# Two-layer graph network on one core: relation products in pairs by Strassen's 7 products for 8, the root product in 35 pieces, 75 edge columns placed by GpSimd's writes

## What is computed

```python
x = layernorm(x + gat_layers(x, src, dst, ...))          # two attention layers, then @ Wu
# relational layer
seg  = edge_type * n + dst
agg  = segment_sum(x[src], seg, 34 * n);  cnt = segment_sum(ones, seg, 34 * n)
mean = agg.reshape(34, n, -1) / maximum(cnt, 1).reshape(34, n, 1)
h1   = einsum('rni,rio->no', mean, W_rel) + x @ W_root + b_rgcn
xw   = h1 @ W_gcn                                         # then a degree-normalised sum over edges
x    = layernorm(x + (sum over edges of xw[src]*norm + xw*dinv^2 + b_gcn))
```

## Time and profile before

| | before |
|---|---|
| median of 3 runs | 3700.54 us |
| the profiled execution | 3701.15 us |
| its span, first to last instruction | 3699.4 us |
| PE / DVE / ACT / POOL busy, share of the span | 93 / 48 / 35 / 33 % |
| DMA | 397.58 MB, mean 107 GB/s |

### The profile page before, as it was taken

How to read it: one execution, slowest core, us unless ns; L and a number is a source line. 1 busy time by engine, 2 the same in 40 slices (tenths; PEclk the granted TensorE clock), 3 DMA queues, 4 the chain that set the end, 5 groups by cost and what they waited for, 6 DMA issues and landing times. The chain is left out here.

```text
span 3699.4 us, 64083 instructions
## 1 busy us (share of the span) xinstructions
PE 3458.5 (93%) x18811; PEld 2178.5 (59%) x18811; DVE 1769.7 (48%) x4227; ACT 1278.9 (35%) x2313; POOL 1227.8 (33%) x1373
## 2 busy tenths in 40 slices
PE   6989988866699999999999999999999998989998
PEld 3544457866466666666666666666666665444545
DVE  8999994767622122111123445544554432443324
ACT  2965535635222222222223444444444432000010
POOL 0000000000055544444502344334433411777771
PEclk9999999987899999999999999999999999999999
DMA  2010010000533333333334555555554544555551
GB/s 86 1 39 0 0 57 24 1 3 9 169 112 105 104 115 107 103 105 104 104 113 130 160 173 167 155 157 172 168 160 152 171 124 134 157 157 158 157 135 54
DMA packets 227146, 397.58 MB, mean 107 GB/s; under 512 B 39186, under 2 KB 179473, under 8 KB 227072
## 3 DMA queue, kind: packets, MB, share of 16 engines
q1 hardware_dynamic: 167226, 253.52, 20.2%
q0 software_dynamic: 57600, 141.81, 14.3%
q10 hardware_dynamic: 2246, 1.29, 0.1%
HBM read 254.24 MB, written 142.25 MB: 107 GB/s over the span
## 5 line engine op out<-in xcount | busy, mean ns | idle before, releaser
L1684 PE MATMUL bank<-arena 128*128 128x384 f16 (+1 forms) x4200 | 1372.1, 327 | 2.2 <-ACT arena L896 2.0
L1685 PE MATMUL bank<-arena 128*128 128x384 f16 (+1 forms) x4200 | 1370.8, 326 | 0.0
L1686 PE MATMUL bank<-arena 128*128 128x384 f16 (+1 forms) x4200 | 1370.8, 326 | 0.0
L896 ACT ACTIVATE arena<-bank,winv 128x384 f32<-128x384 f32 (+1 forms) x680 | 390.5, 579 | 1278.9 <-PE bank L1686 1257.9
L1684 PEld LDWEIGHTS bank<-arena 128*128 128x128 f16 (+2 forms) x4200 | 422.4, 101 | 274.6 <-issue 15.9
L1686 PEld LDWEIGHTS bank<-arena 128*128 128x128 f16 (+2 forms) x4200 | 422.4, 101 | 261.4 <-issue 1.5
L1685 PEld LDWEIGHTS bank<-arena 128*128 128x128 f16 (+2 forms) x4200 | 422.7, 101 | 258.9 <-issue 6.0
L605 POOL DMA_INDIRECT arena<-y_half,idx_now x360 | 401.5, 1115 | 145.1 <-issue 118.0
L589 POOL DMA_INDIRECT w_now<-rel_inv_dram,idx_now x360 | 379.2, 1053 | 155.7 <-issue 87.4
L1320 DVE TENSOR_TENSOR arena<-arena,bank 128x384 f32 x180 | 99.7, 554 | 625.0 <-PE bank L1664 382.8
L619 POOL DMA_INDIRECT arena<-y_half,idx_now x360 | 343.1, 953 | 131.3 <-issue 112.7
(11 more groups left out here) (218 smaller groups left out, 3626.3 us busy)
## 6 DMA issues: line engine op xcount, KB each, us to landing
y_half<-arena SPq DMA_DIRECT2D x612, 192.0 KB
arena<-in_L_gnn_W_rel_dram SPq DMA_DIRECT2D x68, 1152.0 KB, 7.1
arena<-y_half,idx_now POOLq DMA_INDIRECT x720, 3.3
y_half<-arena SPq DMA_DIRECT2D x68, 147.0 KB
w_now<-rel_inv_dram,idx_now POOLq DMA_INDIRECT x360, 2.7
arena<-in_x_dram SPq DMA_DIRECT2D x10, 384.0 KB, 7.3
arena<-in_L_gnn_b_rgcn_dram SPq DMA_DIRECT2D x10, 384.0 KB, 9.2
xu_dram<-arena SPq DMA_DIRECT2D x9, 384.0 KB, 2.6
```

The lines of the kernel that those rows point to most:

```text
L896: nc.scalar.activation(to, bank[n % RB][0:r, 0:CH], ACT.Copy, scale=winv[0:r, c:c + 1]).then_inc(r_copied, 1)
L1684: nc.tensor.matmul(acc, xh, w_hi[c][:, k, :], start=(k == 0), stop=False)
L1685: nc.tensor.matmul(acc, xh, w_lo[c][:, k, :], start=False, stop=False)
L1686: ins = nc.tensor.matmul(acc, xl, w_hi[c][:, k, :], start=False, stop=(k == KT - 1))
```

## The change

1. **Pairs.** A step is now a pair of relations. x1 is cut into 2 x 2 blocks (node tiles 0 to 4 and 5 to 9; depth blocks 0 to 2 and 3 to 5), the weights into 2 x 2 (depth halves; 192-column halves, both relations side by side, so that a product has 384 columns). Seven products (m = 1 to 7) of 5 tile pairs t, 9 matmuls each, replace 2 x 10 tiles of 18. Seven combinations of x1 are made once (`x1_sums`, `x1_high`, `x1_low`), the weight combinations per pair by GpSimd (`t1_t2`, `t3`, `t4`), four `tensor_tensor` of 128 x 1152. Products m = 1, 6, 5, 3 of a tile pair stand one upon the other in one bank, which is read in between; ScalarE copies out after m = 1, 7, 6, 3 (20 a step) and VectorE adds after m = 2, 5, 4 (15 a step).
2. **Weights.** One `w_raw` for the pair (both loads, 1152 KB each, go out when all 7 `low` of the step are done), seven slots of `w_hi`/`w_lo` of 128 x 1152, four maxima of 128 x 1152 instead of two of 128 x 2304.
3. **Edges.** Still six units per pair, for 15 pairs. `weigh` has two buffers, and its last copy (`weighed`) comes one unit later.
4. **Root product.** The same 35 products with W_root as the "pair"; they stand between the first units of the tail (5 before unit 0, then 3 for 2 units, done by unit 20). `cT` is stored to DRAM after the first attention layer and loaded again in the tail (10 DMAs), `hs` of half 1 is set at the tail's start.
5. **Sort.** SCAT = 75 of the 330 columns are left out of the one-hots; GpSimd writes each of their edges (8 bytes) to its place in DRAM with 75 indirect DMAs of 125 rows, SyncE loads the result (360 KB) and VectorE adds it. 17 rounds of 15 columns remain, and the 10 product pieces of L1434 are spread over them.

The diff, cut to its core:

```diff
-        SORT_PARTS = 11
-        SORT_STEPS = EC // NL // SORT_PARTS
+        SORT_STEPS = 1
+        SORT_PARTS = (EC - SCAT) // NL // SORT_STEPS
...
+        ORDER = [(m, t) for ts in ((0, 1), (2, 3), (4,)) for m in (1, 7, 6, 2, 5, 4, 3) for t in ts]
+        BANKS = [(0, 1, 2), (3, 4, 7), (2, 1, 0), (7, 4, 3), (4, 1, 0)]
...
+            pool.wait_ge(units_ready, 1)
+            for c in range(SCAT):
+                nc.gpsimd.indirect_dma_start(
+                    out=placed_dram, out_offset=bass.IndirectOffsetOnAxis(ap=place[:, c:c + 1], axis=0),
+                    in_=pay[:, c, :], in_offset=None).then_inc(edges_placed, 16)
...
+            def t3(q, i):
+                for j in range(2):
+                    pool.wait_ge(w_loaded[j], step(q, i) * 16 + 16)
+                nc.gpsimd.tensor_tensor(X1, B22, B12, ALU.subtract).then_inc(t_done, 1)
+            def t1_t2(q, i):
+                pool.wait_ge(w_max, step(q, i) * 4 + 2)
+                nc.gpsimd.tensor_tensor(B12, B12, B11, ALU.subtract).then_inc(t_done, 1)
+                pool.wait_ge(t_done, step(q, i) * 4 + 2)
+                nc.gpsimd.tensor_tensor(X2, B22, B12, ALU.subtract).then_inc(t_done, 1)
+            def t4(q, i):
+                pool.wait_ge(w_lo_ready, step(q, i) * 7 + LOW[1])
+                nc.gpsimd.tensor_tensor(B11, B21, X2, ALU.subtract).then_inc(t_done, 1)
...
+            def weights_step(q, i, next_q, next_i):
+                weigh(i, 0)
+                t4(q, i)
+                weigh(i, 1)
+                weighed(i, 0)
+                weigh(i, 2)
+                weighed(i, 1)
+                t3(next_q, next_i)
+                t1_t2(next_q, next_i)
+                largest(next_q, next_i)
+                weigh(i, 3)
+                weighed(i, 2)
+                weigh(i, 4)
+                weighed(i, 3)
+                weigh(i, 5)
+                weighed(i, 4)
+                weighed(i, 5)
...
+            # ScalarE, start of a step
+            def one_step(q, i, next_q, next_i, edges):
+                s = step(q, i)
+                if edges:
+                    edge_high(q - 1, i, PER, 0)
+                used_high(q, i, 5, B12, 2)
+                m1_out(s, 0)
+                used_high(q, i, 4, B11, 4)
+                m1_out(s, 1)
+                used_high(q, i, 3, B22, 0)
+                m7_out(s, 0)
...
+            # VectorE, a step, the edge_low / edge_add of six units left out
+                low(q, i, 2, B21)
+                low(q, i, 5, B12)
+                low(q, i, 4, B11)
+                low(q, i, 3, B22)
+                m2_add(s, 0, ybuf[0])
...
+                measure(next_q, next_i, 0)
+                measure(next_q, next_i, 1)
+                m2_add(s, 2, ybuf[2])
+                m2_add(s, 3, ybuf[3])
+                scale(next_q, next_i)
+                m5_add(s, 2, ybuf[2])
...
+            # TensorE, one product
+            def product(s, m, t):
+                for k in range(KH):                      # KH = 3
+                    nc.tensor.matmul(acc, h, w_hi[m - 1][:, k, :], start=fresh and k == 0, stop=False, ...)
+                    nc.tensor.matmul(acc, h, w_lo[m - 1][:, k, :], start=False, stop=False, ...)
+                    ins = nc.tensor.matmul(acc, l, w_hi[m - 1][:, k, :], start=False, stop=k == KH - 1, ...)
+            def m6(s, t):
+                weights(s, 6)
+                copied(s, 1, t)
+                product(s, 6, t)
...
+            # SyncE, a step
+                sp.wait_ge(w_lo_ready, step(q, i) * 7 + 7)
+                load(next_q, next_i)
```

More of the change, by code:

```diff
@@ L235, in program @@
[L235 to L241, removed]
@@ L875, in edge_high @@
+            x1_copy(NT - 1)
+            blocks_high(HT - 1)
+            sums_high(HT - 1)
+            high(0, 0, 2, B21, 0)
             def edge_high(q, i, m, c):
@@ new lines, in _ @@
+            nc.scalar.copy(credit[:, 1:2], ones[:, 0:1]).then_inc(e_hi, 2 * UT)
+            nc.scalar.copy(credit[:, 3:4], ones[:, 0:1]).then_inc(r_copied, COPIES)
+            for i in range(2):
+                act.wait_ge(x1_stored[i], 16 * 2 * XS0[i])
+            with act.Fori(0, PAIRS - 1) as i:
+                one_step(0, i, 0, i + 1, False)
+            one_step(0, PAIRS - 1, 1, 0, False)
+            act.wait_ge(edge_w, UNITS)
+            for c in range(IDXB):
+                next_index(c, c)
@@ L1380, in _ @@
+            roots = 0
+            for u in range(ROOT_UNITS):
+                tail_onehot(0, UNITS, u + 1)
+                for m, t in root_slots(u):
+                    root_out(m, t)
+                edge_add(HALVES - 1, 0, UNITS, u, roots)
+                for m, t in root_slots(u):
+                    if m == 3:
+                        root_add(t, u)
+                        roots += ROOTS
+            first, last = ROOT_UNITS, HALVES - 1
             with dve.Fori(0, REST // 2 - 1) as i:
@@ L1689, in one_step @@
-            def one_step(q, i, j, edges):
-                pe.wait_ge(w_lo_ready, step(q, i, j) + 1)
-                for n in range(NT):
-                    if edges and n in UNIT_AT:
-                        edge_sum(q - 1, i, 2 * PER, j * PER + UNIT_AT.index(n))
-                    pe.wait_ge(r_copied, step(q, i, j) * NT + (n + 1))
-                    product(n, j, bank[n % RB][0:rows(n), 0:CH]).then_inc(r_psum, 1)
-                if edges and NT in UNIT_AT:
-                    edge_sum(q - 1, i, 2 * PER, j * PER + UNIT_AT.index(NT))
@@ L1730, in sums @@
+            with pe.Fori(AGG_PAIRS, PAIRS) as i:
+                one_step(1, i, False)
+            for u in range(ROOT_UNITS):
+                for m, t in root_slots(u):
+                    MAKE[m](STEPS - 1, t)
+                tail_sum(0, UNITS, u)
             def sums(q, j, cs):
```

1021 lines of the change are left out of this document (678 added, 343 removed).

## The result

The changed kernel takes 3866.78 us in the median of 4 runs (3861.28 to 3868.14), the kernel before, beside it, 3700.85 (4 runs): the ratio is 1.0437 (95% interval 1.0424 to 1.0451), 4.4% slower. The forecast was 3530, the range 3455 to 3620. The profiled execution has a span of 3864.8 us against 3699.4.

The account below looks back on a forecast made before the run. The prediction took TensorE to bound the relation products and GpSimd the tail, with GpSimd's chain taking over in q = 0 weigh steps; -90 - 27 - 52 + 8 + 9 - 22 + 4 = -170 from 3701 gave 3530 us, range 3455 to 3620.

Parts of the forecast that it names:

- four sums, 11.2 with their semaphores; the maximum, 0.7. Together 50.0: Weigh steps of q = 0: GpSimd's own work, also six units (35.9) and the last landing (2.2), 50.0 us per step.
- 55.0: Weigh steps of q = 0: GpSimd's 50.0 plus 2.9 of wait and 2.1 of contention, instead of 58.5; -52 us over 15.
- q = 1, 61.0: Steps of q = 1 with edges: 61.0 us instead of 67.0, TensorE's 59.7 plus stalls; -90 us over 15.
- VectorE has per step ... 47 us of 59.7, and none may come late: Steps of q = 1 with edges: VectorE is busy 47 us of TensorE's 59.7, in a queue order walked through.
- x1 loop, +9: x1 stage: 35 VectorE pieces instead of 20 at 0.5 each (+7.5), four GpSimd sums at its end (+3.5), -2 in all; +9 us.
- Sort, -22: Sort: TensorE becomes the bound (-27), GpSimd's writes stay hidden, 4 us of slowed one-hots, 1.5 of small operations; -22 us.
- Rival C: Sort: GpSimd's writes wait until the one-hots end, +96 us, 3626 us in all; chance 8%.
- Plain steps: The four steps without edges: 51.7 us instead of 58.5, with 0.5 for the last tile pair; -27 us.
- Crossing: From q = 0 to q = 1: the first edge sum is needed after 5.8 us instead of 11.7, ends at 15.2; +8 us.
- A: Rival: TensorE bounds everywhere, q = 0 steps 51.7 us and q = 1 steps 60, total 3466 us; chance 24%.
- B: Rival: VectorE's chain with the only w_raw binds q = 1, steps with edges 65 us, +60, total 3590 us; chance 13%.
- D: Rival: VectorE-GpSimd collisions count in full both ways, q = 0 steps 63 us, q = 1 steps 70, total 3824; chance 8%.

Follow-up runs that it names:

- e3: The kernel before with one GpSimd sum of 128 x 1 added ahead of each all-reduce: 1.1049 of the kernel before, 4194 us in a slower batch.
- e1: The changed kernel with GpSimd's all-reduce replaced by a GpSimd copy (other output): 0.9805 of the kernel before, 3720.43 us in a slower batch.
- c3: The changed kernel with the four block sums of a step on VectorE, all-reduce still on GpSimd, in a slower batch: 0.9504 of the kernel before.
- e5: The changed kernel with three of a step's four block sums on VectorE and t4 left on GpSimd: 0.9930 of the kernel before, 3678 us.
- e4: The changed kernel with a step's four block sums and the x1 loop's 20 sums on VectorE: 0.9396 of the kernel before, 3480.44 us.
- c4: The kernel before, unaltered, run again in a slower batch: 3793.9 us.
- e6: The changed kernel with a step's four block sums on VectorE and SCAT = 30 instead of 75, in the faster batch: 3493.24 us.

## Why the prediction was wrong

**The step that failed: GpSimd's own work in a weigh step, "four sums, 11.2 with their semaphores; the maximum, 0.7. Together 50.0".** Each operation was priced right (sums 2.62 against 2.71, the all-reduce 0.40), the passages between them at nothing. They cost 5.7 + 6.8 = 12.5 us per step; 55.0 and 12.5 are 67.5, measured 68.3. e3 shows that they alone make a weigh stage slower, e1 that without them the step is 55.3 (in a slower batch). What the forecast said beside it held: which engine binds, that `high` 4 holds `m1_out(1)`, that TensorE stands before m = 6, released by ScalarE. Whether the 55.0 themselves would be right in the faster batch isn't shown. For 15 steps this is 15 x 13.3 = 200 of the 205 us by which q = 0 was missed.

Could it have been seen before? In the earlier trace rows GpSimd's nine `share` sums (L662) have "11.9 <-issue 11.9", one wait for nothing ahead of the first, and it is the first sum after 70 all-reduces. That looks like the price, but the same idle stands there where no passage does. In the changed kernel the last all-reduce is at 3255.3 and a `t4` follows at 3269.0, so the sum at 3751.75 has sums behind it; e1 has no all-reduce at all. Changed kernel, then e1:

```profile
L823 POOL TENSOR_TENSOR arena<-arena 128x768 f32<-128x768 f32 x9 | 16.3, 1806 | 11.5 <-issue 11.5
...
L823 POOL TENSOR_TENSOR arena<-arena 128x768 f32<-128x768 f32 x9 | 16.5, 1836 | 14.1 <-issue 14.1
```

So that row is another wait, and what it is wasn't tried. The other passage of the kernel before, to its first all-reduce, lies under 51.3 us in which GpSimd waits for VectorE. What its trace had was the name of the event (two records MODIFY_POOL_CONFIG at L581, 924.3, and two at L662, 3574.5) and no row with its price; e3 is the run that would have shown it.

**q = 1, 61.0 against 65.7 (66.8 in the mean).** "VectorE has per step ... 47 us of 59.7, and none may come late": the 47 left out that GpSimd's sums hold VectorE. In the step from 2503 to 2569 us four one-hots cost 2.00 + 2.36 + 2.64 + 2.64 less 4 x 0.28, 8.5 us. The runs put the cause there and not in the reload: q = 1 takes 1105.6 us with four sums and no reload (e1, slower batch; 1014.6 with no sum and no reload in c3, as slow a one), 1029.8 with one sum and both reloads (e5), 1005.3 with neither (e4). So about 90 of the 124 us between e4 and the changed kernel (1129.7) are the sums'. How much is the hold itself and how much that GpSimd's gathers stand behind the sums was not taken apart. VectorE has 5.4 us more to do per step in e4 (four sums of 1.35) and is still not late.

**x1 loop, +9 against +20.** The same omission: "VectorE's pieces grow from 20 to 35 at 0.5 each" was right by count, but they took 0.90; that is 12 us, about the 11 that are missing.

**Sort, -22 against -13.7.** The writes came through as forecast (over at 192, before 207) and VectorE paid more than "4 us of one-hots": some 17. TensorE, whom I made the bound, waits for one-hots. Rival C (the writes starve) did not happen: they start 1.6 us apart beside the one-hots.

**Plain steps** are 53.4 and 53.8 us (51.7 forecast), and in each TensorE stands 2.3 or 2.4 us for an add of VectorE (L1635), where 0.5 was allowed. **Tail** +6.0 (+4). **Crossing**, +8 forecast: TensorE stands 3.3 us for the first edge sum (until 2156.45) and 4.2 and 5.4 for ScalarE's copies (until 2168.49 and 2180.30), 12.9 in all, where the kernel before has 0.6.

**The rivals.** With no sum on GpSimd (e4) the kernel comes to A's numbers, 51.3 and 59.6 per step, 3480 where A said 3466; as A kept the sums where they are, this bears out TensorE's 51.2 and 59.7 and not A's reason. B said 65 per step of q = 1, and 65.7 is near it by luck: from 2300 to 2960 us VectorE waits 2.8 us in all for W_rel, and in e4 its fixed order, with more in it, is not late. D, the slower one, said 3824 and is nearest in time, but only half its mechanism is there. "Each of the four sums holds VectorE as long as it lasts" is what q = 1 and the x1 loop show, and I had written against it that VectorE's durations beside GpSimd barely vary: in the kernel before no sum of GpSimd ran beside them, so those rows could not speak. In q = 0, where D wanted 63 us from collisions, it was the reload. I gave D 8%, and no rival held the passage: the 15 times two passages were in no case, and the range ended at 3620.

## What to carry to other kernels

When work moves to GpSimd, list the kinds of its instructions in order, and price each passage between an all-reduce and an element-wise operation, not only the operations; in a trace, MODIFY_POOL_CONFIG records on its queue mark where such a passage may be. An idle time released by "issue" there is its price only if it goes away without the passage, and a run with one small instruction of the new kind, as e3, measures it. A sum on GpSimd also costs VectorE up to its own length (here 2.6 us) wherever VectorE starts a two-input instruction or a one-hot beside it, so a sum that VectorE does in 1.35 us was cheap here even where VectorE is the busier engine. And a row that says "durations barely vary" is evidence only if the disturbing instruction ran beside it.

## What was not expected of the hardware

Not every change of kind costs a reload: the copy behind the all-reduce starts at once (1529.92 above), and in e1 a sum follows a gather without a gap and the copy a sum. In these kernels only between sum and all-reduce is there one, and gathers and copies that stand between them neither take it nor spare it.

The batches differ where GpSimd's indirect DMAs set the pace. The tail's 360 gathers of the kernel before start over 530 us in a slower one (3130.2 to 3660.7 in c4) and over 451.5 in the faster; its relation stages, which hang on TensorE, differ by 8 us or less, so 79 of the 93 us between its two times lie in the tail. In kernels whose GpSimd has little to spare the weigh steps differ too: 54.4 us (c3) against 51.3 (e6). The cause is open.
